# A ViT tower on one core: the 64-image pipeline written out in full, with orders of its own for the fill

## The reference

```
h = tok(x, W, b, token, pos)                     # (64, 197, 128)
h = h + attn(layernorm(h), Wk, bk, Wv, bv, Wq, bq, Wo, bo)
h = h + ffn(layernorm(h), r_w1, ..., wq0, wk0, wv0, wo0, wq1, ..., wo2)
# attn: state = 0.9*state + 0.1*k v^T ; out_t = q_t @ state_before_t @ Wo + bo
# ffn:  sel = argmax(softmax(relu(mean(x) @ r_w1 + r_b1) @ r_w2 + r_b2)); gqa with set sel
```

## Time and profile before

| | |
|---|---|
| median of 3 runs | 875.6 us (872.46 to 876.5) |
| the profiled execution | span 882.5 us, its own time 884.24 us |
| mean granted TensorE clock | 0.974 of full speed |
| busy, of the span | PE 93%, DVE 69%, ACT 62%, POOL 35% |

### The profile page before, as it was taken

One profiled execution on the slowest core, in us unless ns is written; L12 is line 12 of the kernel. 1 busy time (PEld: TensorE's weight loads), 2 busy tenths in 40 slices (PEclk: granted clock), 3 DMA queues, 4 the chain that ended last, 5 costly groups with the idle time before them and its releaser, 6 DMA issues.

```text
span 882.5 us, 28135 instructions
## 1 busy us (share of the span) xinstructions
PE 821.0 (93%) x9136; PEld 688.8 (78%) x9136; DVE 609.8 (69%) x1960; ACT 550.8 (62%) x1300; POOL 309.2 (35%) x840
## 2 busy tenths in 40 slices
PE   3778799999999999999999998999999999999996
PEld 2657688788888888888888887888888888876774
DVE  3234687777777777777777775777777777778672
ACT  1343457666767677666667774766676667756564
POOL 1364544333433334333433332343344424331100
PEclk9796899999999999999999998999999999999899
DMA  7883776566665656566665755567566656223220
GB/s 164 215 225 113 202 215 189 170 193 185 188 189 181 197 175 191 180 191 188 189 187 177 206 169 159 164 182 199 183 187 189 183 179 206 88 85 126 85 89 19
DMA packets 127080, 150.13 MB, mean 170 GB/s; under 512 B 11710, under 2 KB 121422, under 8 KB 121550
## 3 DMA queue, kind: packets, MB, share of 16 engines
q1 hardware_dynamic: 125250, 147.67, 56.9%
q10 hardware_dynamic: 1676, 0.57, 0.5%
HBM read 30.99 MB, written 6.46 MB: 42 GB/s over the span
## 4 chain that ended last, share of the span: by engine, by line
PE 74%; DVE 9%; issue 6%; POOL 3%; DMA 3%; SPq 2%; POOLq 1%; ACT 1%; DVEq 0%; ACTq 0%
PE ps L433 15%; PE ps L599 10%; PE ps L550 9%; PE ps L576 4%; PE ps L581 4%; PE ps L479 4%; PE ps L522 4%; PE ps L537 3%; PE ps L459 3%; PE ps L631 3%; PE ps L523 2%; PE ps L615 2%; DVE top L816 2%; DVE stats L729 1%; PE ps L468 1%
## 5 line engine op out<-in xcount | busy, mean ns | idle before, releaser
L816 DVE TENSOR_REDUCE top<-ps 99x2 f32<-99x394 f32 x512 | 264.9, 558 | 103.3 <-PE ps L550 102.7
L939 ACT ACTIVATE prob<-ps 99x396 f32<-99x396 f32 x512 | 227.3, 496 | 99.3 <-PE ps L581 94.6
L433 PE MATMUL ps<-w_tok,cols 126*99 126x128 f32 x1280 | 175.6, 289 | 2.6 <-ACT cols L894 2.5
L433 PEld LDWEIGHTS ps<-w_tok,cols 126*99 126x99 f32 x1280 | 155.1, 176 | 9.2 <-issue 2.9
L894 ACT ACTIVATE cols<-img 126x588 f32<-126x588 f32 (+1 forms) x128 | 135.3, 1058 | 10.3 <-DMA img<-img 10.2
L550 PE MATMUL ps<-stack 64*99 64x198 f32 x1024 | 111.2, 296 | 10.8 <-DVE top L816 3.7
L550 PEld LDWEIGHTS ps<-stack 64*99 64x99 f32 x1024 | 64.6, 162 | 68.7 <-issue 40.5
L576 PE MATMUL ps<-top_rows,pick_rows 64*99 64x198 f32 x1024 | 114.5, 255 | 1.6 <-ACT prob L939 1.5
L599 PE MATMUL ps<-prob,v_ones 99*32 99x198 f32 (+1 forms) x2048 | 113.9, 340 | 0.4 <-ACT prob L939 0.4
L581 PE MATMUL ps<-stack 64*99 64x198 f32 x1024 | 113.6, 253 | 0.0
L576 PEld LDWEIGHTS ps<-top_rows,pick_rows 64*99 64x99 f32 x1024 | 85.3, 163 | 3.8 <-ACT prob L939 2.2
(11 more groups left out here) (146 smaller groups left out, 1513.9 us busy)
## 6 DMA issues: line engine op xcount, KB each, us to landing
stack<-qk SPq DMA_DIRECT2D x256, 198.0 KB, 2.8
img<-in_x SPq DMA_DIRECT2D x192, 150.1 KB
img<-img SPq DMA_DIRECT2D x64, 449.4 KB
img<-img SPq DMA_DIRECT2D x64, 448.5 KB
out<-h SPq DMA_DIRECT2D x64, 49.5 KB
out<-h SPq DMA_DIRECT2D x64, 49.0 KB
w_rows<-in_L_tok_W SPq DMA_DIRECT2D x1, 294.0 KB, 3.3
sets<-in_L_ffn_wo SPq DMA_DIRECT2D x3, 64.0 KB
```

What stands on the lines that cost most here:

```text
L433: last = nc.tensor.matmul(ps[0:T, CX, t * D:(t + 1) * D], cols[b.ring % 2][:, s, t * T:(t + 1) * T], w_tok[0:KROWS, s, :], start=(s == 0), ...
L816: nc.vector.tensor_reduce(top[:, c // 4, first:first + 2], columns, AX.X, ALU.max, negate=True).then_inc(m_read, 1)
L939: nc.scalar.activation(prob[:, c, :], ps[0:T, E0 + c % 2, 0:CHUNK], ACT.Exp, scale=DK ** -0.5).then_inc(exp_done, 1)
```

## The change

- `run_slots` is a plain Python loop over all slots: no hardware loop, every wait and address a constant.
- SP fetches the weight sets in slots 2 to 4 and the routing weights in slot 4.
- GpSimd builds one weight set at the end of each of its slots 6, 7 and 8 (`build_set(0)` to `(2)`); the first waits for all 16 weight DMAs.
- ScalarE no longer waits for the last setup matmul ahead of its first slot. The copies of w_kq and w_vo, and the waits for the pads, stand in `patch_columns(1, 0)`, behind the waits for image 1. TensorE waits for `w_vo_ready` in the first `turn_normed1`.
- TensorE, VectorE and ScalarE have plans of their own for slots 0 to 11.

```diff
-def run_slots(engine, slot, lag):
-
-    for n in range(PEEL):
-        slot(Image(n // RING, n % RING))
-    with engine.Fori(PEEL // RING, B // RING) as turn:
-        for u in range(RING):
-            slot(Image(turn, u))
-    for n in range(B, B + lag):
+def run_slots(slot, lag):
+
+    for n in range(B + lag):
         slot(Image(n // RING, n % RING))
...
-                if isinstance(n.round, int) and 3 <= n.i < 3 + len(KV):
-                    ffn_weights(n.i - 3)
-                if isinstance(n.round, int) and n.i == 3 + len(KV):
+                if 2 <= n.i < 2 + len(KV):
+                    ffn_weights(n.i - 2)
+                if n.i == 2 + len(KV):
                     routing_weights()
...
-            def build_sets():
-                pool.wait_ge(ffn_in, 16 * 16)
-                for i, n in enumerate(KV):
+            def build_set(i):
+                if i == 0:
+                    pool.wait_ge(ffn_in, 16 * 16)
+                for n in KV[i:i + 1]:
...
-                if isinstance(n.round, int) and n.i == ROUTED - 2:
-                    build_sets()
-            run_slots(pool, slot, TOPPED)
+                if ROUTED - len(KV) <= n.i < ROUTED:
+                    build_set(n.i - ROUTED + len(KV))
+            run_slots(slot, TOPPED)
...
             pe.wait_ge(w_tok_ready, 1)
-            pe.wait_ge(w_vo_ready, 1)
...
+                else:
+                    pe.wait_ge(w_vo_ready, 1)
...
-                for step, b, *which in plan:
+                filling = [
+                    (patches, patched, 0), (attend_out, added), (patches, patched, 1), (turn_normed1, turned),
+                    (project_z, turned), (route_hidden, routing), (scores, turned), (route_logits, routing),
+                    (project_qk, projected), (weigh, turned), (turn_normed2, added),
+                ]
+                for step, b, *which in filling if n.i < MAXED else plan:
...
+                if n.i < MAXED:
+                    plan = [(choose, choosing), (add_attention, added), (tokens, patched), (route_relu, routing),
+                            (mask_scores, turned), (route_bias, routing), (normalise2, added), (low_halves, projected)]
...
-            act.wait_ge(pe_step, 4)
-            nc.scalar.activation(w_kq[:, :], ps[:, CZ, 0:D], ACT.Copy)
-            nc.scalar.activation(w_vo[:, :], ps[:, CZ, D:2 * D], ACT.Copy).then_inc(w_vo_ready, 1)
-            act.wait_ge(x_pads_ready, 1)
             act.wait_ge(cols_padded, 2)
-            act.wait_ge(ones_set, 1)
...
+                    if b.i == 1:
+                        act.wait_ge(pe_step, 4)
+                        nc.scalar.activation(w_kq[:, :], ps[:, CZ, 0:D], ACT.Copy)
+                        nc.scalar.activation(w_vo[:, :], ps[:, CZ, D:2 * D], ACT.Copy).then_inc(w_vo_ready, 1)
+                        act.wait_ge(x_pads_ready, 1)
+                        act.wait_ge(ones_set, 1)
...
+                if n.i < MAXED:
+                    plan = [(keep_x1t, turned), (keep_z, turned), (patch_columns, shifted, 0), (keep_x2t, added),
+                            (route_exp, routing), (high_halves, projected), (patch_columns, shifted, 1), (keep_u, turned)]
```

More of the change, by code:

```diff
@@ L33 @@
 RING = 16
-PEEL = 32
 BATCH = 4
@@ L276, in slot @@
                         step(b)
-                if isinstance(n.round, int) and 3 <= n.i < 3 + len(KV):
-                    ffn_weights(n.i - 3)
-                if isinstance(n.round, int) and n.i == 3 + len(KV):
+                if 2 <= n.i < 2 + len(KV):
+                    ffn_weights(n.i - 2)
+                if n.i == 2 + len(KV):
                     routing_weights()
-            run_slots(sp, slot, STORED)
+            run_slots(slot, STORED)
             for j in range(RING):
@@ L313, in build_sets @@
                     if n == HEADS:
-                        nc.gpsimd.tensor_copy(into_k, raw[i][1][:, :].rearrange("p (h a d) -> p a d h", a=2, d=DK))
+                        last = nc.gpsimd.tensor_copy(into_k, raw[i][1][:, :].rearrange("p (h a d) -> p a d h", a=2, d=DK))
                         continue
@@ L324, in build_sets @@
                 last.then_inc(sets_built, 1)
-                pool.wait_ge(sets_built, 1)
+                pool.wait_ge(sets_built, i + 1)
             def weights_of(b):
@@ L651, in slot @@
                 ]
-                for step, b, *which in plan:
+                filling = [
[4 more added lines that the diff above has]
+                for step, b, *which in filling if n.i < MAXED else plan:
                     if b.exists():
                         step(b, *which)
-            run_slots(pe, slot, ENDING)
+            run_slots(slot, ENDING)
         @block.vector
@@ L862, in slot @@
                         step(b, *which)
-            run_slots(dve, slot, ENDING)
+            run_slots(slot, ENDING)
         @block.scalar
@@ L982, in slot @@
                         step(b, *which)
-            run_slots(act, slot, ENDING)
+            run_slots(slot, ENDING)
 def build(nc, ins, out):
```

## The result

The changed kernel takes 884.6 us (median of 6 runs, 879.7 to 886.6) against 874.9 us for the kernel before (6 runs, 871.4 to 877.8): ratio 1.0101, 95% interval 1.0063 to 1.014. It is slower by 1%, some 9.7 us by the medians. Forecast was 880, +4.3. By the ratio it is 8.8 us.

A forecast was written before the change was run, and what follows sets the result against it. TensorE was taken to bound the steady slots, unchanged, leaving the loop's turn and the fill. -6.6 (turn) + 2.9 (slots) + 11 (clock) - 3 (given back) = +4.3 us on the 875.6 median: 880 us, range 867 to 886.

The forecast's parts named there:

- The loop's turn: At the loop's one backward jump: straight code removes TensorE's pause and the low clock after it, gaining 6.6 us.
- Rival 3: The straight program pauses as often for its instructions, so the turn's pause comes back elsewhere: 887 us, chance 0.07.
- The uncovered chain: Slots from 5 on end with turn_normed2, x2t, column part 1: 1.7 us, nothing covering it; slots of 8.4 us.
- The clock in the fill: Slots 6 to 11: the clock falls once in nearly every slot, 1.85 us each, +11 us (bounds 0 and 22).
- Rival 1: The clock stays high in the fill, since no single wait passes 1.4 us: 869 us, faster; chance 0.25.
- rival 2: The clock falls in about every second fill slot, +5.5 us instead of 11: 874 us, chance 0.2.
- The signs that did not come: In the fill: clock 0.50 over more than half of 48 to 110 us, first max_scores near 110 us.
- The weight sets: POOL's copies, split over three slots, hide behind each slot's end; 4.5 us of POOL work leave the path.
- "given back" at slots 12 and 13: After the fill, its greater length gives the DMA queue time: 3 us taken back (bounds 1 and 4).
- the forecast's +2.9: The fill's slots at full clock: first max_scores 2.9 us later than 96.36, longer slots partly offset by the set stall.
- First image: At the start: an earlier image 0 gains nothing; two copies ahead of image 1's columns cost +0.5 us.

The follow-up runs named there:

- experiment 3: The kernel before with its loop of two passes written as two one-pass loops, so no jump back: 870.5 us, ratio 0.995 to the kernel before.
- Experiment 6: The changed kernel with four unread matmuls behind turn_normed2 in slots 5 to 11: 871.9 us, ratio 0.9968 to the kernel before.
- experiment 5: The changed kernel with ScalarE's column part 1 right behind part 0 and keep_x2t last in the fill: 863.3 us, ratio 0.9846 to the kernel before.
- experiment 7: The kernel before with straight code, weights fetched a slot earlier and sets built in three slots: 868.3 us, ratio 0.9911 to the kernel before.
- Experiments 4: The changed kernel with the old orders of TensorE, VectorE and ScalarE in the fill: 867.5 us, ratio 0.9895 to the kernel before.

## Why the prediction was right, and where it was off

*Right in sign and range, 880 against 884.6, and the mechanisms are those it named. The size is in part luck: two of its signs did not come, and its terms err both ways.* By its own terms:

- **The loop's turn, -6.6.** Straight code alone measured -7.0; the jump back is the cause (experiment 3). Rival 3, that the pause comes back elsewhere, is out: no pause in any straight trace.
- **The uncovered chain.** Forecast as 1.35 us of idle PE a slot in slots of 8.4 us; measured 1.28 and 8.16 at full clock, at the end of every slot from 5 on (up to 1.68 where high_halves stands in it). Over the whole kernel some 9 to 11 us.
- **The clock in the fill, +11.** Measured 12.7, or 11.6 by the ratios, against a kernel that keeps two short falls. In the profiled execution it fell six times between 51 and 106 us, about every 10 us, the first at 51.4 us, right behind a stretch with 1.83 us of 3.40 busy. Each time the slot lasted 1.5 us longer or more. Rival 1 is out, and so is rival 2 (a fall in every second slot): five of the six slots had one. Experiment 6 shows that the falls are a cost of their own and no mark of the chain. Short idles that come often were enough here. The Trainium skill's page TensorE: Matmul & The Clock Gate, section A second HAM failure mode: psum-queue depth-cycling, tells of a clock that swings behind frequent short idles; these rows agree. The section HAM oscillation — how this bites in real kernels, on the same page of the Trainium skill, speaks of long gaps only; the row at 51.40 shows 0.50 with no wait above 1.4 us ahead of it.
- **The signs that did not come.** The prediction wanted a clock of 0.50 over more than half of 48 to 110 us and the first max_scores near 110 (99 for rival 1). Its own trace has a mean of 0.83 there, so a third of the time, and max_scores at 100.37. Busy time by stretch, the changed kernel and then the kernel before:

```profile
48.00:110.00 62.00, 46.19 (x276) 40.29 (x276) 26.00 (x102) 21.51 (x49) 29.83 (x85) 0.83 0.57 158
48.00:110.00 62.00, 46.95 (x309) 40.81 (x309) 32.11 (x117) 24.34 (x54) 32.05 (x94) 0.85 0.67 178
```

  Slot 6 began at 43.62, not 47.1 (patches of slot 5 ran at full pace), and the six slots to max_scores took 56.8 us, not 63.2. The two traces differ little in the clock (0.83 and 0.85), because the forecast's +11 was put on top of rows in which it had already fallen; the second trace of the kernel before has 0.92 over the same stretch. The 12.7 us are against experiment 6, not against the kernel before.
- **The weight sets, and "given back" at slots 12 and 13.** This step was mis-sized. The new slots 6 to 11 add up to 12.0 us more than six of 6.7, with 0.5 for the first image; the forecast's +2.9 thus credits 9.6 us for what the fill of before loses to the sets' stall, the low clock and the routing. With 3 us behind the fill that makes 12.6. The kernel with new orders and without the chain has both credits, and it is 6.3 us below straight code (863.3 and 869.6). From the tokens of slot 12 to those of slot 16 the profiled execution took 152.85 - 107.76 = 45.1 us, before 146.89 - 100.77 = 46.1: 1 us given back, not 3. The clock over 100 to 140 us averaged 0.87, against 0.91 before; it fell again at 102.6 and at 119.7. Timeline of DVE, before and then after:

```profile
100.77 0.42 DVE L725 TENSOR_TENSOR h<-ps,add_rows 99x256 f32<-99x256 f32 x1
...
146.89 0.42 DVE L725 TENSOR_TENSOR h<-ps,add_rows 99x256 f32<-99x256 f32 x1
...
107.76 0.42 DVE L726 TENSOR_TENSOR h<-ps,add_rows 99x256 f32<-99x256 f32 x1
...
152.85 0.42 DVE L726 TENSOR_TENSOR h<-ps,add_rows 99x256 f32<-99x256 f32 x1
```

  The claim that split copies hide behind a slot holds with the new orders, where normalise2 and turn_normed2 come last, even in the slots of 6.64 us of experiment 5 (there scores waits 0.40 us for route_relu). With the old orders they don't hide (experiment 7).
- **First image, +0.5.** cols(0) began at 16.37 instead of 16.91, patches(1) at 28.02 instead of 28.43, so not later, and other traces vary by more. Experiments 4 and 7 differ in this alone: 0.9895 and 0.9911, not to be told apart.

The sum then reads: straight code -7.0, new orders and sets without the chain -6.3, chain +8.6, clock +12.7: +8.0 on 876.6. These are differences along a row of kernels from the one before to the changed one, so they must add up to the measured time; that they do proves nothing. By the ratios they are -6.7, -6.7, +10.7 and +11.6, +8.8 in all.

The forecast's sign rested on the clock, as it said. It took its rows from a trace that it knew to be 1% slower than the median (mean clock 0.974), and put their difference on the median; what it didn't ask is which rows were slow by chance. The trace of after turned out a lucky one.

## What to carry to other kernels

When an engine's order is rewritten, look for a step that waits for the other engine's *last* step and stands ahead of what the other engine needs *first*: here two instructions behind the wrong one made a chain across the slot's end that nothing could cover, and moving keep_x2t behind the columns was worth 21 us. On TensorE price such a wait twice, once as time and once as clock, and test the second by filling the wait with matmuls that nobody reads. And don't compare two kernels by one trace each: the order of the two profiled executions was the reverse of that of the medians.

## What the runs showed of the hardware

- **A jump back over 16 slots of code costs 6.6 us once:** 3.3 us in which TensorE stands (3.57 in the second trace), then the same again through 6.8 us at 1.2 GHz. A loop of one pass, with its registers, has no pause in its trace (865.4 us, straight code 865.2).
- **The same wait brings a fall in some executions and none in others.** In the drain TensorE waits 1.2 us for DVE's row maxima in all twelve traces. In both traces of the kernel before, the clock fell behind it; in the ten others, all without the jump back, it did not. Two against ten is no proof that the jump matters so far behind it, and nothing here shows why. Busy time by stretch, the kernel before:

```profile
811.50:815.50 4.00, 2.66 (x42) 1.88 (x39) 3.31 (x12) 2.15 (x6) 1.25 (x5) 1.00 0.65 214
815.50:822.30 6.80, 6.80 (x50) 5.25 (x46) 2.45 (x7) 2.95 (x7) 1.36 (x5) 0.50 0.04 11
```

and the same wait in the changed kernel, timeline of PE, with no fall after it:

```profile
811.50 0.43 PE L546 MATMUL ps<-stack 64*99 64x198 f32 x4 [1.19 <-DVE top L817]
```

- **The spread of the timed runs follows the clock in part.** In the kernel before and the changed one, the slower executions have the lower mean clock. In experiments 5 and 6 the two don't go together: in experiment 5 864.2 us has 0.998 and 860.7 has 0.992. Time at the low level is 2 x (1 - mean clock) x span, less than the true one where the start isn't told (above). Over the timed runs it averages 40.6 us for the changed kernel, 28 to 31 for the kernel before, 16.7 for experiment 5 and 14.7 for experiment 6.
